# Four column groups for the router's product, and x's scale from sums on ScalarE

## The chip, the cores and the metric

The kernel runs on one core of one Trainium2 chip. The metric is device time in microseconds (us), the median of several executions. A core has TensorE (matmuls, written PE), VectorE (DVE), ScalarE (ACT), GpSimd (POOL) and SyncE (SP), which run their own instruction streams and meet at semaphores, and 16 DMA engines that they share.

## The reference

4096 tokens of 512 features pass through an adapted linear layer and then through a mixture-of-experts layer, with a residual:

```python
cond   = x @ W.T + ((x @ A[idx].T) @ Bm[idx].T) * scalings[idx]
shared = sum over 2 experts of gelu(cond @ Wsh_up[e]) @ Wsh_down[e]
probs  = softmax(cond @ W_router)                 # 512 x 16
gate   = the two largest of probs, zero elsewhere
routed = sum over 16 experts of gate[e] * gelu(cond @ Wrt_up[e]) @ Wrt_down[e]
out    = x + shared + routed
```

## The kernel before

The work has four stages: the linear layer with the router's logits, a shared-expert stage in which the tokens are also sorted by expert, the routed experts in 79 tiles of 128 tokens, and the rest of the shared experts with the sum of everything. The change lies in the first stage and its end.

The first stage goes over 16 chunks `c` of 256 tokens (`c = 2i + s`, where `s` picks one of two buffers), each of two tiles of 128 tokens. All matmuls but the router's, the adapters' second one and the transposes have two float16 parts for each float32 operand, `x` among them: `x` times a power of two is rounded to float16 (the high part, ScalarE, `high_x`), and what is left is the low part (VectorE, `x_low`); products run in three passes (high*high, high*low, low*high). The router's product is in float32, so that the choice of experts is right.

The first two chunks are an exception: their linear products are taken in float32, straight from the loaded weights.

TensorE's order is written out by hand. Step `c` (`cond_step`, L1301) is: `adapter_inputs(c)` (L1261), `cond_products(c, 0)` for the chunk's first tile (L1272), `cond_transposes(c-1)` (L1288), `cond_products(c, 1)`, `router_products(c-1)` (L1297), `adapter_products(c)` (L1280). The router's product takes 128 tokens of the transposed chunk `hid` as the stationary operand and 16 columns of the router's matrix `wr` as the moving one, four of them summed in PSUM for each tile. The routed weights, 16 experts, arrive by DMA in steps 0 to 6, and ScalarE and VectorE look for their scale in steps 0 to 7 (`lot_sums` with sums of absolute values at L643, `lot_maxima` at L881) and split them into parts in steps 8 to 15 (`high_routed` at L612, `low_routed` at L906, two experts in a step, each as an up and a down part).

The other engines' order in a step:

- ScalarE: `high_x(c+1)` (L654), `cond_T(c-1)` (L675, the transposes out of PSUM into `hid`), `lot_sums` or two `high_routed`, `cond_rows(c)` (L666, the linear layer's result out of PSUM into `rows`).
- VectorE: `mask_xa(c)` (L851), `row_max(c-1)` (L874), `x_low(c+1)` (L935), `x_largest` of chunk `c+2` (L918, then L920, which keeps the exponent), a weight piece, `x_scales(c+2)` (L925 to L929), a weight piece, `top(c-1)` (L859 to L869, the two best experts).
- GpSimd: one `partition_all_reduce` (L523) for chunk `c+2`, between `x_largest` and `x_scales`.
- SyncE: loads `x` of chunk `c+3`, up to two experts' weights, and stores `rows` and `hid`.

At the end of the stage SyncE reloads the first chunks of `hid` as `condT` for the shared experts (L394; chunk 1's load waits until all routed weights are split, since it lands behind them), ScalarE and VectorE split them (`high_condT` L633, `low_condT` L1002), and TensorE's order, after step 15, is: `shared_up` block 0 of chunk 0 (L1349), `cond_transposes(15)`, blocks 1 and 2, `router_products(15)`, block 3, block 0 of chunk 1, `prefix_products` (L1325), which needs the choice of experts of all tokens (VectorE's `top(15)` and one-hot matrices, L1050 to L1052).

## Time and profile before

| | us |
|---|---|
| median of 3 runs | 653.16 |
| lowest and highest | 651.33, 656.0 |
| the profiled execution | 656.53 |
| its span (first to last instruction) | 654.8 |
| mean granted clock of TensorE | 0.989 |

The profiled execution is one more run of the same program. Its span leaves out what lies before the first and after the last instruction, 1.73 us together. The rows of the trace come from it.

### The profile page before, as it was taken

The page shows a single profiled execution, that of the slowest core. Times are in us where ns is not written, and L with a number is a line of the kernel's source. Part 1 is how long each engine was busy: PE and PEld are TensorE (multiplying, and loading weights), DVE is VectorE, ACT ScalarE, POOL GpSimd, SP SyncE. Part 2 cuts the span into 40 slices and gives each one's busy share as a digit, 9 for nine tenths or more (in the row PEclk, how much of TensorE's full clock was granted, in tenths as well). Part 3 has the DMA queues.
Part 4 walks back from the last instruction along what each step waited for, and adds up shares of the span by engine and source line. Part 5 has one row for each costly group of instructions (what it writes and reads, how often), then busy time and mean ns, then how long its engine had stood idle before and what let it go on. Part 6 is the DMA issues. An engine that isn't in the chain of part 4 may idle for free.

```text
span 654.8 us, 13547 instructions
## 1 busy us (share of the span) xinstructions
PE 622.5 (95%) x4116; PEld 430.7 (66%) x4117; DVE 427.6 (65%) x820; ACT 323.4 (49%) x487; POOL 180.8 (28%) x270
## 2 busy tenths in 40 slices
PE   4999999999999999799999999999999998989794
PEld 2466666666676786477777777777777775756461
DVE  2768989999879963455555555555555534688774
ACT  0356567676766322255555555555555543333230
POOL 1000000000001002333333333333333227777770
PEclk8999999999999999999999999999999999999898
DMA  7699964444243423545555555555555459999976
GB/s 281 273 375 422 422 234 145 149 142 153 111 165 116 154 72 128 193 143 161 161 161 160 160 160 160 160 160 160 160 160 160 144 186 393 327 316 331 360 214 248
DMA packets 49477, 135.62 MB, mean 207 GB/s; under 512 B 6000, under 2 KB 6000, under 8 KB 47024
## 3 DMA queue, kind: packets, MB, share of 16 engines
q1 hardware_dynamic: 38016, 97.86, 39.9%
q0 software_dynamic: 11440, 37.50, 21.0%
q8 instruction: 11, 0.18, 0.1%
q14 instruction: 10, 0.08, 0.0%
HBM read 86.31 MB, written 49.02 MB: 207 GB/s over the span
## 4 chain that ended last, share of the span: by engine, by line
PE 71%; POOL 11%; DVE 6%; issue 6%; DMA 5%; ACT 1%; SPq 0%; POOLq 0%; DVEq 0%; ACTq 0%
PE bank L1440 16%; PE bank L1421 15%; PE bank L1272 12%; POOL rtw L579 10%; PE bank L1405 5%; PE bank L1280 4%; PE bank L1297 4%; PE bank L1261 3%; PE bank L1362 3%; PE bank L1430 3%; PE bank L1349 3%; PE bank L1288 2%; PE bank L1335 1%; DMA region<-w_r 1%; DMA rtw<-r_dram,row_idx 1%
## 5 line engine op out<-in xcount | busy, mean ns | idle before, releaser
L1149 DVE SCALAR_TENSOR_TENSOR region<-bank,scale,region 128x512 f16<-128x512 f32 x79 | 59.4, 751 | 114.1 <-ACT region L785 114.1
L1440 PE MATMUL bank<-rtw,tmp 128*128 x474 | 116.5, 382 | 3.0 <-DVE tmp L1157 3.0
L1421 PE MATMUL bank<-rtw,region 128*128 x948 | 116.6, 273 | 0.0
L1421 PEld LDWEIGHTS bank<-rtw,region 128*128 128x128 f16 x948 | 92.9, 98 | 10.2
L1362 PE MATMUL bank<-shw,hid 128*128 128x512 f16 x384 | 87.9, 384 | 8.5 <-DVE rtw L1216 7.8
L554 POOL DMA_INDIRECT region<-xc_dram,slot_idx x79 | 77.8, 985 | 61.3 <-POOL slot_idx L551 61.3
L1349 PE MATMUL bank<-act_in,shw 128*128 128x256 f16 x768 | 87.9, 273 | 1.7 <-issue 1.4
L1349 PEld LDWEIGHTS bank<-act_in,shw 128*128 128x128 f16 x768 | 74.8, 98 | 14.8 <-issue 2.2
L792 ACT ACTIVATE region<-bank,un_dn 128x512 f32<-128x512 f32 x79 | 54.3, 687 | 59.1 <-PE bank L1440 59.1
L579 POOL DMA_INDIRECT rtw<-r_dram,row_idx x64 | 71.5, 1117 | 27.8 <-issue 16.6
L1440 PEld LDWEIGHTS bank<-rtw,tmp 128*128 128x128 f16 x474 | 46.6, 98 | 42.1 <-issue 4.6
L1362 PEld LDWEIGHTS bank<-shw,hid 128*128 128x128 f16 x384 | 37.5, 99 | 52.5 <-DVE rtw L1216 6.9
L781 ACT ACTIVATE tmp<-bank,un_up 128x256 f32<-128x256 f32 x79 | 37.4, 474 | 64.3 <-PE bank L1421 64.3
L551 POOL COPY slot_idx<-tok 128x1 int32 (+1 forms) x79 | 15.3, 194 | 158.7 <-PE bank L1405 116.7
L785 ACT ACTIVATE region<-bank,scale 128x512 f16<-128x512 f32 x79 | 54.3, 687 | 6.0 <-PE bank L1405 6.0
L743 ACT ACTIVATE tmp<-bank,un_up 128x256 f32<-128x256 f32 x44 | 20.3, 471 | 72.0 <-PE bank L1349 52.9
L1191 DVE SCALAR_TENSOR_TENSOR rtw<-rtw,gate 128x512 f32 (+1 forms) x64 | 45.3, 749 | 14.8 <-DMA rtw<-r_dram,row_idx 10.2
L1405 PE MATMUL bank<-ident,region 128*128 128x128 f32 x316 | 47.5, 273 | 0.6 <-DMA region<-xc_dram,slot_idx 0.6
L906 DVE SCALAR_TENSOR_TENSOR rtw<-rtw,scale 128x1024 f16<-128x1024 f32 x32 | 39.7, 1280 | 6.5 <-ACT rtw L612 6.5
L1155 DVE TENSOR_SCALAR tmp<-bank,to_mid 128x256 f16<-128x256 f32 x79 | 38.2, 484 | 7.9 <-PE bank L1430 4.6
L523 POOL PARTITION_ALL_REDUCE x_max_all<-x_max x14 | 4.9, 352 | 128.2 <-DVE x_max L920 128.2
L1157 DVE SCALAR_TENSOR_TENSOR tmp<-bank,to_mid,tmp 128x256 f16<-128x256 f32 x79 | 38.2, 484 | 2.8
(156 smaller groups left out, 834.7 us busy)
## 6 DMA issues: line engine op xcount, KB each, us to landing
r_dram<-region SPq DMA_DIRECT2D x79, 256.0 KB
rtw<-rt_w SPq DMA_DIRECT2D x16, 1024.0 KB, 11.4
act_in<-xT SPq DMA_DIRECT2D x16, 512.0 KB, 4.1
xc_dram<-rows SPq DMA_DIRECT2D x16, 512.0 KB, 3.0
xcT_dram<-hid SPq DMA_DIRECT2D x16, 512.0 KB, 2.9
rtw<-x_rows SPq DMA_DIRECT2D x16, 512.0 KB, 4.5
rtw<-xcT_dram SPq DMA_DIRECT2D x13, 512.0 KB
out<-rtw SPq DMA_DIRECT2D x9, 512.0 KB
```

The lines of the kernel that those rows point to most:

```text
L554: nc.gpsimd.indirect_dma_start(out=xg[s], out_offset=None, in_=xc_dram, in_offset=bass.IndirectOffsetOnAxis(ap=slot_idx[s][:].bitcast(U32) ...
L579: nc.gpsimd.indirect_dma_start(out=routed_row(slot, r, t), out_offset=None, in_=r_dram, in_offset=bass.IndirectOffsetOnAxis(ap=row_idx[slo ...
L785: nc.scalar.activation(xgT[s][:, 0], R_XT[s][:].rearrange("p (k t) -> p k t", k=HK), ACT.Copy, scale=col(scale, C_ALL).bitcast(F32)).then_ ...
L792: nc.scalar.activation(rrow[s], R_DN[s][:], ACT.Copy, scale=col(un_dn, ROUTED)).then_inc(rrow_ready, 1)
L1149: nc.vector.scalar_tensor_tensor(xgT[s][:, 1], R_XT[s][:].rearrange("p (k t) -> p k t", k=HK), col(scale, C_ALL).bitcast(F32), xgT[s][:, 0 ...
L1191: last = nc.vector.scalar_tensor_tensor(y, routed_row(slot, r, t), gate[:, r, bass.ds(c * NT + t, 1)], y, ALU.mult, ALU.add)
L1272: last = mm(COND[NT * s + t][:], act_in[s][:, k, at] if whole else xp[s][:, ap, k, at], w_in[:, k, :] if whole else wt[:, bp, k, :], start ...
L1349: last = mm(UP[em % 2][:, 0:CHUNK], shw[:, e, w0:w0 + P], actT[s][:, xp, k, :], start=(k == 0 and n == 0), stop=(k == HK - 1 and n == 2))
L1362: last = mm(DOWN[t][:], hidT[s][:, xp, em, t * P:(t + 1) * P], shw[:, em // DM, w0:w0 + H], start=(em == 0 and n == 0), stop=(em == EM - 1 ...
L1405: last = nc.tensor.transpose(R_XT[s][:, k * P:(k + 1) * P], xg[s][:, k * P:(k + 1) * P], ident[:])
L1421: last = mm(R_UP[s][:, 0:D], xgT[s][:, xp, k, :], rtw[:, bass.ds(e, 1), w0:w0 + D].rearrange("p a d -> p (a d)"), start=(k == 0 and n == 0 ...
L1440: last = mm(R_DN[s][:], midT[s][:, xp, m, :], rtw[:, bass.ds(e, 1), w0:w0 + H].rearrange("p a h -> p (a h)"), start=(m == 0 and n == 0), s ...
```

## The change

The router's matrix becomes the stationary operand: each of its four pieces (128 features x 16 experts, padded with zeros to 32 columns) stands in column group `k` of the array, and the 256 tokens move. The four products are no longer summed in PSUM: product `k` writes PSUM partitions 32k to 32k+31 (`LOGIT_T`). ScalarE copies this to `lt` (`logit_T`), and a second product (`router_sums`, one for each tile of 128 tokens) with the constant matrix `fold` as moving operand sums the four groups and turns the result back to tokens x experts, for `top` as before. `router_sums(c-2)` stands behind `adapter_inputs(c)`, so `top(c-1)` of VectorE waits into TensorE's next step.

The scale of `x` no longer comes from the largest absolute value on VectorE but from the sum of absolute values of each partition on ScalarE (`x_sums`, in `cond_rows`), of which the largest over the partitions is taken as before; the exponent is now cut out behind GpSimd's reduction, by one more small operation in `x_scales`. `x_scales` and the weight pieces of VectorE change places. GpSimd pads `wr` with zeros, and the DMA that loads it now writes pieces of 64 bytes (16 columns of every 32) where it wrote 256 bytes for each partition. The parts of the diff that only size buffers and declare semaphores are left out (`GROUP` is 32, `fold` is 128 x 16, `lt` 128 x 256).

```diff
@@ -173,6 +175,8 @@
         ident = sb("ident", [P, P])
         lower = sb("lower", [P, P], BF16)
+        fold = sb("fold", [P, E_RT])
+        lt = sb("lt", [P, CHUNK])
         ones = sb("ones", [P, P], BF16)
         iota_p = xam[1][:].bitcast(F16).rearrange("p (l n) -> p l n", n=GRP // 2)
         iota_e = sb("iota_e", [P, E_RT])
...
@@ -243,6 +247,7 @@
         bank = [ctx.enter_context(nc.psum_tensor(f"bank{i}", [P, 512], F32)) for i in range(8)]
         XA, COND, XPOSE, LOGIT = bank[0], bank[1:3] + bank[6:8], bank[3:5], bank[5]
+        LOGIT_T, LOGIT = LOGIT[:, 0:CHUNK], LOGIT[:, CHUNK:CHUNK + NT * E_RT]
         PRE, TOT, INV, TILE_E = bank[6], bank[7], bank[0], bank[5]
         UP, DOWN = bank[1:3], bank[3:5]
         R_XT, R_UP, R_MT, R_DN = [bank[0], bank[5]], bank[6:8], bank[2:0:-1], bank[3:5]
...
@@ -339,7 +345,7 @@
             sp.dma_start(flat(act_in[0][:]), chunk_T(xT, 0)).then_inc(act_loaded[0], 16)
             sp.dma_start(sc_col[:], scal).then_inc(w_mask, 16)
             sp.dma_start(idx_b[:], idx.partition_broadcast(P)).then_inc(w_mask, 16)
-            for dst, src in ((w_in, WT), (bmt, BmT), (wr, w_r)):
+            for dst, src in ((w_in, WT), (bmt, BmT), (wr[:, :, 0:E_RT], w_r)):
                 sp.dma_start(dst, src).then_inc(w_cond, 16)
             sp.dma_start(flat(act_in[1][:]), chunk_T(xT, 1)).then_inc(act_loaded[1], 16)
             sp.dma_start(arrived(0), sh_up).then_inc(w_shared, 16)
@@ -502,6 +508,7 @@
                            allow_small_or_imprecise_dtypes=True).then_inc(iotas, 1)
             nc.gpsimd.iota(tok_no[:], [[P, TT]], base=-TOK // 2, channel_multiplier=1,
                            allow_small_or_imprecise_dtypes=True).then_inc(iotas, 1)
+            nc.gpsimd.memset(wr[:, :, E_RT:GROUP], 0.0).then_inc(wr_padded, 1)
             nc.gpsimd.memset(ident[:], 0.0).then_inc(masks, 1)
             nc.gpsimd.memset(ones[:], 1.0).then_inc(masks, 1)
             nc.gpsimd.memset(lower[:], 1.0).then_inc(masks, 1)
@@ -519,8 +526,8 @@
             def x_reduce(c, s):
-                pool.wait_ge(x_max_ready, c - 1)
-                nc.gpsimd.partition_all_reduce(x_max_all[s][:], x_max[s][:], P, RMAX).then_inc(x_reduced, 1)
+                pool.wait_ge(x_sum_ready, c - 1)
+                nc.gpsimd.partition_all_reduce(x_sum_all[s][:], x_sum[s][:], P, RMAX).then_inc(x_reduced, 1)
             reduce_max(1, LIN_W, SH_UP)
             reduce_max(2, SH_UP, RT_UP)
@@ -653,11 +660,19 @@
                 act.wait_ge(act_used, c - 1)
                 nc.scalar.activation(xp[s][:, 0], act_in[s][:], ACT.Copy, scale=x_scale[s][:].bitcast(F32)).then_inc(x_half, 1)
-            def cond_rows(i, s, first=False):
+            def x_sums(i, s):
+                act.wait_ge(act_loaded[s], 16 * (i + 2))
+                nc.scalar.activation(rows[s][:].rearrange("p t h -> p (t h)"), flat(act_in[s][:]), ACT.Abs,
+                                     accum_out=x_sum[s][:]).then_inc(x_sum_ready, 1)
+
+            def cond_rows(i, s, first=False, more=True):
                 c = 2 * i + s
                 if not first:
                     act.wait_ge(rows_stored[s], 16 * i)
                     act.wait_ge(c_chunk_ready, c - 1)
+                if more and not (first and s == 0):
+                    x_sums(i, s)
+                    act.wait_ge(x_sum_ready, c + 1)
                 for t in range(NT):
                     act.wait_ge(cond_ready, NT * c + t + 1)
                     if first:
@@ -675,25 +690,37 @@
                     nc.scalar.copy(hid[s][:, :, t * P:(t + 1) * P],
                                    XPOSE[t][:].rearrange("p (k t) -> p k t", k=HK)).then_inc(condT_ready, 1)
+            def logit_T(c, first=False):
+                act.wait_ge(lt_psum, c + 1)
+                if not first:
+                    act.wait_ge(logit_ready, c)
+                nc.scalar.copy(lt[:], LOGIT_T).then_inc(lt_ready, 1)
+
             def cond_step(i, s, first=False):
                 c = 2 * i + s
                 cond_T(c - 1, i - 1 + s, 1 - s, first)
+                logit_T(c - 1, first)
                 cond_rows(i, s, first and s)
             act.wait_ge(scale_ready, 1)
             high_linear(wt[:, 0], w_in, LIN_W)
             high_linear(at_[:, 0], at_in, LIN_A)
             cond_rows(0, 0, first=True)
+            act.wait_ge(act_loaded[0], 2 * 16)
+            nc.scalar.activation(hid[0][:].rearrange("p k t -> p (k t)"), flat(act_in[0][:]), ACT.Abs,
+                                 accum_out=x_sum[0][:]).then_inc(x_sum_ready, 1)
             high_x(2, 0)
             cond_step(0, 1, first=True)
             high_x(3, 1)
             cond_T(1, 0, 1, first=True)
+            logit_T(1)
             lot_sums(1)
             act.wait_ge(scale_ready, 2)
             high_shared(0)
             cond_rows(1, 0)
             high_x(4, 0)
             cond_T(2, 1, 0)
+            logit_T(2)
             lot_sums(3)
             high_shared(1)
             cond_rows(1, 1)
@@ -701,13 +728,14 @@
                 for s in range(2):
                     high_x(2 * i + s + 1, 1 - s)
                     cond_T(2 * i + s - 1, i - 1 + s, 1 - s)
+                    logit_T(2 * i + s - 1)
                     if i == 2:
                         lot_sums(5 + 2 * s)
                     else:
                         for e in (9 + 4 * s, 11 + 4 * s):
                             lot_sums(e)
                     cond_rows(i, s)
-            def routed_step(i, s, more=True):
+            def routed_step(i, s, more=True, more_x=True):
                 c = 2 * i + s
                 if more:
                     high_x(c + 1, 1 - s)
@@ -715,12 +743,14 @@
                     high_condT(0, 0, C_EARLY, early=True)
                     nc.scalar.activation(warm[:], sc_col[:], ACT.Gelu)
                 cond_T(c - 1, i - 1 + s, 1 - s)
-                for e in range(2):
-                    high_routed(2 * c - NC + e)
-                cond_rows(i, s)
+                high_routed(2 * c - NC)
+                logit_T(c - 1)
+                high_routed(2 * c - NC + 1)
+                cond_rows(i, s, more=more_x)
             high_x(NC // 2 + 1, 1)
             cond_T(NC // 2 - 1, A_HALF // 2 - 1, 1)
+            logit_T(NC // 2 - 1)
             act.wait_ge(scale_ready, 3)
             for e in range(2):
                 high_routed(e)
...
@@ -757,7 +787,9 @@
             gelus(0, 0, SH_FIRST, early=True, blocks=range(1))
             cond_T(NC - 1, A_HALF - 1, 1)
             high_condT(1, 1, C_EARLY, early=True)
-            gelus(0, 0, SH_FIRST, early=True, blocks=range(1, EM))
+            gelus(0, 0, SH_FIRST, early=True, blocks=range(1, 3))
+            logit_T(NC - 1)
+            gelus(0, 0, SH_FIRST, early=True, blocks=range(3, EM))
             high_hid(0, 0, SH_FIRST, early=True)
             gelus(1, 1, SH_FIRST, early=True, blocks=range(1))
             high_condT(2, 0, C_EARLY, early=True)
...
@@ -913,16 +945,12 @@
                 low(part(DN_LO), arrived(e + 1)[:, WU:], RT_DN, part(DN_HI), 2 * e + 4)
-            def x_largest(i, s):
-                dve.wait_ge(act_loaded[s], 16 * (i + 1))
-                nc.vector.tensor_reduce(x_max[s][:], flat(act_in[s][:]), AX_X, ALU.max, apply_absolute_value=True).then_inc(x_max_found, 1)
-                dve.wait_ge(x_max_found, 2 * i + s - 1)
-                nc.vector.tensor_scalar(x_max[s][:].bitcast(I32), x_max[s][:].bitcast(I32), 255 * EXP_ONE, None,
-                                        ALU.bitwise_and).then_inc(x_max_ready, 1)
-
             def x_scales(c, s):
                 dve.wait_ge(x_reduced, c - 1)
-                nc.vector.tensor_scalar(x_expo[s][:], x_max_all[s][:].bitcast(I32), float(30 * EXP_ONE), None,
+                nc.vector.tensor_scalar(x_expo[s][:], x_sum_all[s][:].bitcast(I32), 255 * EXP_ONE, None,
+                                        ALU.bitwise_and).then_inc(x_expo_found, 1)
+                dve.wait_ge(x_expo_found, c - 1)
+                nc.vector.tensor_scalar(x_expo[s][:], x_expo[s][:], float(30 * EXP_ONE), None,
                                         ALU.max).then_inc(x_expo_ready, 1)
                 dve.wait_ge(x_expo_ready, c - 1)
                 nc.vector.tensor_scalar(x_unscale[s][:], x_expo[s][:], float(-TOP * EXP_ONE), None, ALU.add)
@@ -947,20 +975,17 @@
                     mask_xa(c, s)
                 row_max(c - 1, 1 - s)
                 x_low(c + 1, 1 - s)
-                if masked:
-                    lot_maxima(lots[0])
-                x_largest(i + 1, s)
-                for at in lots[1:2] if masked else lots[0:1]:
+                for at in lots:
                     lot_maxima(at)
                 x_scales(c + 2, s)
-                for at in lots[2:] if masked else lots[1:]:
-                    lot_maxima(at)
                 top(c - 1, 1 - s)
             def low_linear(dst, src, n, hi, half):
                 dve.wait_ge(lin_half, half)
                 nc.vector.scalar_tensor_tensor(dst, src, col(scale, n).bitcast(F32), hi, ALU.mult, ALU.subtract).then_inc(lin_split, 1)
+            dve.wait_ge(consts, 1)
+            nc.vector.tensor_reduce(fold[:], ident[:].rearrange("p (k e) -> p e k", k=HK)[:, 0:E_RT, :], AX_X, ALU.add).then_inc(fold_ready, 1)
             mask_xa(0, 0)
             dve.wait_ge(w_cond, 3 * 16)
             dve.wait_ge(w_adapters, 16)
...
@@ -1025,14 +1049,12 @@
                 row_max(c - 1, 1 - s)
                 if c + 1 < NC:
                     x_low(c + 1, 1 - s)
-                if more:
-                    x_largest(i + 1, s)
                 if c + 1 == NC:
                     low_early(0)
                 low_routed(2 * c - NC)
+                low_routed(2 * c - NC + 1)
                 if more:
                     x_scales(c + 2, s)
-                low_routed(2 * c - NC + 1)
                 top(c - 1, 1 - s)
             for i in range(A_HALF // 2, A_HALF):
@@ -1292,14 +1314,20 @@
                 pe.wait_ge(condT_ready, NT * c + NT)
                 if not first:
                     pe.wait_ge(logit_copied, c)
+                for k in range(HK):
+                    last = mm(LOGIT_T[k * GROUP:(k + 1) * GROUP, :], wr[:, k, :], hid[s][:, k, :], start=True, stop=True)
+                last.then_inc(lt_psum, 1)
+
+            def router_sums(c):
+                pe.wait_ge(lt_ready, c + 1)
                 for t in range(NT):
-                    for k in range(HK):
-                        last = mm(LOGIT[:, t * E_RT:(t + 1) * E_RT], hid[s][:, k, t * P:(t + 1) * P], wr[:, k, :],
-                                  start=(k == 0), stop=(k == HK - 1))
+                    last = mm(LOGIT[:, t * E_RT:(t + 1) * E_RT], lt[:, t * P:(t + 1) * P], fold[:], start=True, stop=True)
                 last.then_inc(logit_ready, 1)
-            def cond_step(c, i, s, first=False):
+            def cond_step(c, i, s, first=False, sums=True):
                 adapter_inputs(c, i, s, whole=first)
+                if sums:
+                    router_sums(c - 2)
                 cond_products(c, s, 0, whole=first)
                 cond_transposes(c - 1, 1 - s, first)
                 cond_products(c, s, 1, whole=first)
@@ -1313,9 +1341,19 @@
             for t in range(NT):
                 cond_products(0, 0, t, whole=True)
             adapter_products(0, 0)
-            cond_step(1, 0, 1, first=True)
+            pe.wait_ge(wr_padded, 1)
+            pe.wait_ge(fold_ready, 1)
+            cond_step(1, 0, 1, first=True, sums=False)
             pe.wait_ge(lin_split, 2)
-            with pe.Fori(1, A_HALF) as i:
+            adapter_inputs(2, 1, 0)
+            router_sums(0)
+            cond_products(2, 0, 0)
+            cond_transposes(1, 1)
+            cond_products(2, 0, 1)
+            router_products(1, 1)
+            adapter_products(2, 0)
+            cond_step(3, 1, 1)
+            with pe.Fori(2, A_HALF) as i:
                 cond_step(2 * i, i, 0)
                 cond_step(2 * i + 1, i, 1)
@@ -1366,10 +1404,12 @@
             pe.wait_ge(w_split, 2)
             pe.wait_ge(rows_ready, TT - NT)
             shared_up(0, 0, first=True, blocks=range(1))
+            router_sums(NC - 2)
             cond_transposes(NC - 1, 1)
             shared_up(0, 0, first=True, blocks=range(1, 3))
             router_products(NC - 1, 1)
             shared_up(0, 0, first=True, blocks=range(3, EM))
+            router_sums(NC - 1)
             shared_up(0, 1, blocks=range(1))
             prefix_products()
             shared_up(0, 1, blocks=range(1, 3))
```

## Rows read from the trace of the kernel before

**Rows 1.** The profile page: busy time of each engine, and the DMA line of the 40 slices

```profile
PE 622.5 (95%) x4116; PEld 430.7 (66%) x4117; DVE 427.6 (65%) x820; ACT 323.4 (49%) x487; POOL 180.8 (28%) x270
...
DMA  7699964444243423545555555555555459999976
```

**Rows 2.** One step: length, PE, PEld, DVE, ACT, POOL busy us; clock, DMA share, GB/s

```profile
109.32:120.18 10.86, 10.86 (x67) 6.97 (x66) 10.21 (x24) 7.74 (x10) 0.35 (x1) 1.00 0.40 145
```

**Rows 3.** Chain that ended last, one step of the stage: start us, us, engine

```profile
109.32 1.69 PE bank L1297 x16
111.01 1.81 PE bank L1280 x4
112.82 1.31 PE bank L1261 x12
114.13 2.59 PE bank L1272 x12
116.72 0.87 PE bank L1288 x8
```

**Rows 4.** The same chain, the first steps

```profile
3.61 8.85 DMA region<-w_r
...
22.90 1.74 PE bank L1261 x8
...
31.97 0.97 ACT hid L675 x2
32.98 1.96 PE bank L1297 x16
```

**Rows 5.** TensorE in order of time (start us, us): the product with one stationary column

```profile
219.89 0.30 PE L1330 MATMUL bank<-ident,tile_col 128*1 128x82 f32 x2
220.13 2.79 PE L1349 MATMUL bank<-act_in,shw 128*128 128x256 f16 x24
```

**Rows 6.** Groups by line and shape, 0 to 260 us: busy us, mean ns, idle before

```profile
L918 DVE TENSOR_REDUCE x_max<-act_in 128x1 f32<-128x1024 f32 x14 | 17.0, 1214 | 7.1 <-DMA act_in<-xT 7.0
...
L743 ACT ACTIVATE tmp<-bank,un_up 128x256 f32<-128x256 f32 x24 | 10.9, 470 | 36.7 <-PE bank L1349 30.3 <-DVE hid L1010 6.4
L643 ACT ACTIVATE rtw<-rtw 128x1024 f16<-128x1024 f32 x10 | 10.5, 1057 | 0.2
```

**Rows 7.** ScalarE in order of time, one step

```profile
122.97 1.44 ACT L666 ACTIVATE rows<-bank,un_cond 128x512 f32<-128x512 f32 x2
124.31 1.14 ACT L654 ACTIVATE arena<-act_in,x_scale 128x1024 f16<-128x1024 f32 x1
128.06 1.07 ACT L675 COPY hid<-bank 128x512 f32<-128x512 f32 x2 [2.61 <-PE bank L1288]
```

**Rows 8.** TensorE in order of time, end of the stage

```profile
185.22 1.85 PE L1297 MATMUL bank<-region,hid 128*128 128x16 f32 x16
...
199.15 0.39 PE L1325 MATMUL bank<-arena,lower 128*128 128x512 bf16 x1 [1.13 <-DVE arena L1052]
```

**Rows 9.** ScalarE in order of time, end of the stage

```profile
185.92 2.35 ACT L612 ACTIVATE rtw<-rtw,scale 128x1024 f16<-128x1024 f32 x2 [0.32 <-DVE rtw L906]
...
194.59 0.82 ACT L743 ACTIVATE tmp<-bank,un_up 128x256 f32<-128x256 f32 x2
```

**Rows 10.** VectorE in order of time, end of the stage

```profile
184.60 4.98 DVE L906 SCALAR_TENSOR_TENSOR rtw<-rtw,scale 128x1024 f16<-128x1024 f32 x4 [2.07 <-ACT rtw L612]
...
195.92 0.18 DVE L859 COPY lg_c<-bank 128x32 f32<-128x32 f32 x1
...
197.21 1.42 DVE L1050 TENSOR_TENSOR arena<-iota_e,chosen 128x512 bf16<-128x512 f32 x2
```

**Rows 11.** SyncE's queue in order of time, end of the stage

```profile
189.61 0.35 SPq L394 DMA_DIRECT2D rtw<-xcT_dram  x1
```

**Rows 12.** VectorE in order of time, third step

```profile
47.67 1.22 DVE L918 TENSOR_REDUCE x_max<-act_in 128x1 f32<-128x1024 f32 x1 [5.03 <-DMA act_in<-xT]
```

**Rows 13.** ScalarE in order of time, third step

```profile
46.88 1.46 ACT L666 ACTIVATE rows<-bank,un_cond 128x512 f32<-128x512 f32 x2 [0.71 <-PE bank L1280]
```

More of the change, by code:

```diff
@@ L25 @@
 AR = N_AD * RANK
+GROUP = 32
+assert HK * GROUP == P and E_RT <= GROUP
 assert AR == P
@@ L124, in adaln_moe_kernel @@
         midT = [tmp[:, (2 + s) * D:(3 + s) * D].bitcast(F16).rearrange("p (a m t) -> p a m t", a=2, m=DM) for s in range(2)]
-        region = sb("region", [P, HK * H + HK * AR + H + HK * E_RT])
+        region = sb("region", [P, HK * H + HK * AR + H + HK * GROUP])
         def carve(sizes):
@@ L144, in carve @@
                 views.append(v)
-            assert at <= HK * H + HK * AR + H + HK * E_RT
+            assert at <= HK * H + HK * AR + H + HK * GROUP
             return views
-        wt, at_, bmt, wr = carve([((2, HK, H), F16), ((2, HK, AR), F16), ((H,), F32), ((HK, E_RT), F32)])
+        wt, at_, bmt, wr = carve([((2, HK, H), F16), ((2, HK, AR), F16), ((H,), F32), ((HK, GROUP), F32)])
         acc0, acc1, pref = carve([((TT, E_RT), F32)] * 3)
@@ L227, in adaln_moe_kernel @@
         un_up, to_mid, un_dn = sb("un_up", [P, 3]), sb("to_mid", [P, 3]), sb("un_dn", [P, 3])
-        x_max = [sb(f"x_max{s}", [P, 1]) for s in range(2)]
-        x_max_all = [sb(f"x_max_all{s}", [P, 1]) for s in range(2)]
+        x_sum = [sb(f"x_sum{s}", [P, 1]) for s in range(2)]
+        x_sum_all = [sb(f"x_sum_all{s}", [P, 1]) for s in range(2)]
         x_expo = [sb(f"x_expo{s}", [P, 1], I32) for s in range(2)]
@@ L261, in adaln_moe_kernel @@
         lin_half, lin_split = sem("lin_half"), sem("lin_split")
-        x_max_found, x_max_ready, x_reduced = sem("x_max_found"), sem("x_max_ready"), sem("x_reduced")
+        x_sum_ready, x_reduced, x_expo_found = sem("x_sum_ready"), sem("x_reduced"), sem("x_expo_found")
         x_expo_ready, x_scale_ready = sem("x_expo_ready"), sem("x_scale_ready")
@@ L270, in adaln_moe_kernel @@
         logit_ready, logit_copied, best_ready = sem("logit_ready"), sem("logit_copied"), sem("best_ready")
+        wr_padded, fold_ready, lt_psum, lt_ready = sem("wr_padded"), sem("fold_ready"), sem("lt_psum"), sem("lt_ready")
         place_found, top_ready = sem("place_found"), sem("top_ready")
@@ L732, in _ @@
             for s in range(2):
-                routed_step(A_HALF - 1, s, more=s == 0)
+                routed_step(A_HALF - 1, s, more=s == 0, more_x=False)
             def gelus(c, s, n=SH_REST, early=False, blocks=range(EM)):
@@ L858, in top @@
                 dve.wait_ge(logit_ready, c + 1)
-                nc.vector.tensor_copy(lg_c[s][:], LOGIT[:, 0:NT * E_RT].rearrange("p (t e) -> p t e", t=NT)).then_inc(logit_copied, 1)
+                nc.vector.tensor_copy(lg_c[s][:], LOGIT.rearrange("p (t e) -> p t e", t=NT)).then_inc(logit_copied, 1)
                 dve.wait_ge(logit_copied, c + 1)
@@ L981, in _ @@
             link(nc.vector.tensor_scalar(mask[:], mask[:], w_to_a[:], None, ALU.mult))
-            x_largest(1, 0)
             x_scales(2, 0)
```

## The prediction

> **What bounds the kernel now.** I read the page first: TensorE is busy 95% of the span and no other engine passes 66% [rows 1]. Since that is an average over four stages, I then took busy time by stretch for one step of the stage that changes. A step lasts 10.87 us; TensorE is busy for all of it, VectorE for 10.2 us and ScalarE for 7.7 us [rows 2]. So TensorE sets the pace and VectorE stands 0.65 us behind it: a saving on TensorE alone would soon stop at VectorE. The chain of waits says the same: it runs through TensorE's five pieces of a step without a gap, 1.69 (router) + 1.81 (adapters) + 1.31 + 2.59 twice + 0.87 (transposes) = 10.86 us [rows 3]. Two places are not TensorE's: in steps 0 to 5 the DMA engines are nearly full as well (nines in the slices from 33 to 82 us [rows 1]), and at the end of the stage the chain goes through ScalarE, VectorE and a DMA before it comes back to TensorE [rows 8 to 11].
>
> **TensorE, the first router product.** Removed: 16 records in 1.69 us, one per 106 ns [rows 3]: each of 8 float32 products is two records, and each streams only 16 columns, so the stationary loads set the time. Added: 4 products with 256 moving columns, 8 records. The trace has this very shape with the full array, the adapters' float32 product of chunk 1: 8 records of 256 columns in 1.74 us, 0.218 us a record [rows 4]. That is the upper bound, if the groups don't overlap: the streamed columns cost more than the loads that were saved. The lower bound is two records, 0.44 us, if all four groups run together. No row of the trace shows two matmuls at once. I take 5 records, 1.09 us, by this mechanism: the two records of a product use the same columns of the array and can't overlap; if records start in the order of the program, group 1's first starts beside group 0's second, and so on, so each further product adds one record: 2+1+1+1. It lies between the ends, and I choose it since the records of this trace on TensorE always start in program order.
>
> The page "TensorE: Matmul & The Clock Gate" of the Trainium skill, Part 3, says that matmuls on different column groups run concurrently with starts about 4 ns apart, and that matmuls nevertheless start and end in strict order. No run here shows either yet; the first half of the rule alone would make the product about one product long, the lower bound, and the second half is what speaks for 5 records.
>
> **TensorE, the second product and the switches.** `router_sums` is 2 float32 products, 4 records with 128 stationary columns, 16 moving: at 106 ns each [rows 3] 0.42 us. Going into the grouped form and out of it may cost time too. The nearest row is the product with one stationary column: two records of 82 columns, which at 256 columns in 0.218 us need 0.14 us, but the next line starts 0.24 us after them [rows 5]. I take these 0.10 us for each switch, 0.20 us a step, with 0 and 0.3 us a step as bounds.
>
> The page "TensorEngine Tiling (Array Packing)" of the Trainium skill, under Key Properties, says that changing the tiling mode drains TensorE. It gives no time; the 0.10 us of that row agree with its direction, and the sum doesn't need the rule.
>
> Step: -1.69 + 1.09 + 0.42 + 0.20 = +0.02 us. Up to the transposes of chunk 14, where the end of the stage takes over, there are 14 of them: +0.3 us.
>
> **VectorE and ScalarE in the steps.** VectorE loses the largest value, 1.21 us [rows 6], and its mask goes to x_scales: some 9.0 us are left of 10.87. ScalarE gains x_sums: 1.06 us [rows 6] and some 0.2 us to read the accumulator; and logit_T, 128x256 out of PSUM, 0.47 us like the GELU of that shape [rows 6]: 7.7 + 1.7 = 9.4 us. Both fit. What matters is the new wait on ScalarE: logit_T stands between the two high_routed and waits for the router's product, and x_sums stands ahead of cond_rows. From the product's end E: 0.1 + 0.42 (copy) + 2.3 (second high_routed) + 1.25 (x_sums) + 0.1 + 1.34 (rows [rows 7]) puts `rows` at E+5.5. The transposes that need them start after the switch, 1.81 + 1.31 + 0.42 + 2.59 us [rows 3], at E+6.2: 0.7 us of slack, where before the idle of 2.6 us ahead of the copies [rows 7] and more was there. Then high_x takes it to E+6.6, before the next transposes are out. VectorE: x_scales wait for the sums (E+4.5), top(c-1) for router_sums; x_low follows high_x (E+6.6) and row_max and is out at some E+9.0, while adapter_inputs need it at E+12.7. Cost nothing, as long as the 0.7 us hold.
>
> GpSimd's reduction is as long as before and still has no one but x_scales behind it. SyncE's queue is unchanged in order; its stores follow `rows` and `hid`, up to 2 us later in a step, hidden, since the same buffer is written again two steps (21.7 us) on.
>
> **The first steps.** The load of w_r ends the wait for the first products (8.85 us [rows 4]); it now writes 512 pieces where there were 128, 24 more for each DMA engine: some 0.3 us, 0 to 0.5. On the other side, router(0) waited until 32.98 for the copies that stood behind x's scale on VectorE [rows 4]; ScalarE can sum chunk 2 while VectorE still splits weights: -0.6 us. Chunk 4's x lands at 47.67, behind the routed weights [rows 12]; rows(2) were copied at 46.88 [rows 13] and now stand behind the sum of chunk 4: 47.7 + 1.25 + 0.1 + 1.34 = 50.3. The transposes of chunk 2 came at 51.36 and come at some 50.7 now: no wait. With 0.65 us less a step they would come at 49 and lose about 1 us.
>
> **The end of the stage.** The chain there: the last low_routed (184.60, four, to 189.5 [rows 10]), the DMA of chunk 1 (189.61 [rows 11]), its high part, the GELU of block 1 (to 195.0 [rows 9]), block 3. The second pair of high_routed started at 185.92 [rows 9]. Now it waits for logit_T(14): the product starts at 185.22 [rows 8], + 0.1 + 1.09 + 0.1 + 0.42 = 186.95, so the last low_routed, the DMA and the GELU are 0.9 us later: 195.9. Then block 3, 1.31; router_sums(15) with a switch, 0.52; top(15), which had started at 195.92 [rows 10], now only here: 1.3; the one-hot matrices, 1.9 [rows 10]: 201.0. prefix_products started at 199.15 with 1.13 us of waiting [rows 8]. +1.8 us. The 0.6 + 0.6 us that the two last router products may save here are swallowed by that wait. Everything behind it hangs on TensorE and moves along.
>
> **Sum:** 0.3 + 0.3 - 0.6 + 1.8 = +1.8 us, on the profiled execution 656.5 to 658.3. That execution lies 3.4 us over the median of 653.16; on the median: 655.0. Its own range, from no switches and no cost of the load (-2.8 - 0.3) to 0.3 us of switches and 2 us more at the end: 651 to 659.
>
> **Rivals.** (1) The four groups overlap wholly: 0.44 us in place of 1.09, 0.65 us less a step, 14 steps: -9.1, and the end 0.6 us less late, against 1 us lost at the transposes of chunk 2: 646.3, without switches 643.5. For it: the groups share neither columns nor PSUM partitions. Against it: two records for each product, in order. It is only to be had since VectorE, at 9.0 us, now fits under a step of 10.2. (2) Slower: the groups don't overlap at all, so that the change doesn't do what it says. 8 records, 1.74 us: +0.65 us a step, +9.1, and 0.6 us more at the end: 664.7, without switches 662. It decides from the point where the records of the product take over 1.3 us. For it: every matmul of this trace has the array alone. (3) ScalarE becomes the bound: if its waits add more than 0.7 us between E and rows, TensorE waits for `rows` ahead of each transposes. Price for 0.5 us over it, in the 6 steps with both high_routed and x_sums: +3 us, 658; it can come on top of each case.
>
> **Chances.** The forecast 0.38, whole overlap 0.32, none 0.25, ScalarE's bound 0.05. A run of this kernel tells about 1% (6.5 us) from no change. Faster by over 1% (under 646.6): a bit over half of the first rival, 0.2. Slower by over 1% (over 659.7): the second and the edge of the third, 0.28. Within 1%: 0.52. The range goes from 644 to 665, since the bounds of the unknown overlap lie that far apart and neither rival can be left out.
>
> **What would show it.** The distance from the start of the grouped products to adapter_products: 0.5, 1.1 to 1.2 or 1.8 us. A step of 10.2, 10.9 or 11.6 us. ScalarE's copy of `lt` about 0.1 us behind the product's end; no idle of TensorE ahead of the transposes but for chunk 2; prefix_products' wait grown from 1.1 to over 2 us. The forecast is wrong first of all if the records of one product overlap each other or if those of different groups don't, next if a switch costs several tenths.

## The result, and the profile after

The changed kernel takes 652.51 us (median of 12 runs, 648.17 to 655.01). The kernel before, run 12 times beside it, takes 654.11 us (650.85 to 657.67). The ratio is 0.9958, with an interval of 0.9939 to 0.9977: some 2.7 us faster (the medians lie 1.6 us apart). The forecast was 655.0, a slight loss; the time lies inside its range, and on the other side of no change. The profiled execution has a span of 651.2 us.

The page after, busy time by engine:

```profile
PE 615.5 (95%) x4052; PEld 410.8 (63%) x4053; DVE 412.5 (63%) x807; ACT 341.9 (53%) x531; POOL 181.5 (28%) x271
```

TensorE has lost 7.0 us of busy time and VectorE 15.1, ScalarE has gained 18.5 [rows 1]; the share of TensorE is still 95%. The chain of waits, one step, as in [rows 3] (start us, us, engine; the first row is the high part of the step before):

```profile
126.76 2.59 PE bank L1294 x12
129.35 0.57 PE bank L1318 x8
129.92 1.91 PE bank L1302 x4
131.83 1.31 PE bank L1283 x12
133.14 0.35 PE bank L1324 x4
133.50 2.60 PE bank L1294 x12
136.10 0.87 PE bank L1310 x8
```

The chain still runs through TensorE alone. The router's 1.69 us [rows 3] have become 0.57 (grouped products) and 0.35 (router_sums), and adapter_products read 1.91 for 1.81. The chain counts from end to end; by starts adapter_products are as long as before (1.82 and 1.80 us), and the 0.09 us stand ahead of the product. The step is 10.21 us, 0.66 less. Busy time by stretch of that step, columns as in [rows 2]:

```profile
129.92:140.13 10.21, 10.21 (x62) 5.64 (x61) 9.55 (x24) 9.12 (x12) 0.50 (x1) 1.00 0.44 155
```

TensorE is full; VectorE's busy time fell from 10.21 us [rows 2] to 9.55 (9.2 to 9.6 in the steps after it), and it still fits, 0.66 us under the step.

Fourteen steps of 0.66 and 0.7 us at router(0) would be some 10 us. To see where they went I follow the starts of the transposes. TensorE in order of time, before: transposes of chunk 0 and of chunk 14, first matmul of the routed stage:

```profile
27.90 1.04 PE L1288 MATMUL bank<-ident,rows 128*128 128x128 f32 x8
...
181.76 1.04 PE L1288 MATMUL bank<-ident,rows 128*128 128x128 f32 x8
...
275.11 2.74 PE L1440 MATMUL bank<-rtw,tmp 128*128 x6 [3.03 <-DVE tmp L1157]
```

And after, with the three that wait longest between them (in brackets the idle time ahead and what ended it):

```profile
29.34 1.04 PE L1310 MATMUL bank<-ident,rows 128*128 128x128 f32 x8
...
92.96 1.16 PE L1310 MATMUL bank<-ident,rows 128*128 128x128 f32 x8 [0.54 <-ACT rows L681]
...
104.00 1.16 PE L1310 MATMUL bank<-ident,rows 128*128 128x128 f32 x8 [0.54 <-ACT rows L681]
...
115.39 1.16 PE L1310 MATMUL bank<-ident,rows 128*128 128x128 f32 x8 [0.90 <-ACT rows L681]
...
176.77 1.04 PE L1310 MATMUL bank<-ident,rows 128*128 128x128 f32 x8
...
272.90 1.77 PE L1480 MATMUL bank<-rtw,tmp 128*128 x6 [3.02 <-DVE tmp L1179]
```

The stretch from chunk 0 to chunk 14 fell from 153.86 to 147.43 us, 6.4 and not 10: in the steps 2 to 8 TensorE waits for ScalarE's `rows`. From chunk 14 to the routed stage it grew from 93.35 to 96.13 us, 2.8 us given back. The rest is not the change's: the routed stage itself lasts as long (256.2 us in both up to the start of the last stage), and the last stage, which no edit touches, lasted 120.4 to 125.3 us in the profiles of this study (130.0 in e1, whose choice of experts is another).

ScalarE in the step of the first of these waits:

```profile
86.32 0.37 ACT L697 COPY lt<-bank 128x256 f32<-128x256 f32 x1 [2.49 <-PE bank L1318]
86.59 1.06 ACT L650 ACTIVATE rtw<-rtw 128x1024 f16<-128x1024 f32 x1
...
90.98 1.04 ACT L665 ACTIVATE rows<-act_in 128x1024 f32<-128x1024 f32 x1
...
92.15 1.27 ACT L681 ACTIVATE rows<-bank,un_cond 128x512 f32<-128x512 f32 x2
```

`logit_T` stands first in this step, so ScalarE idles 2.49 us for the product and only then takes four weight pieces (lot_sums) and x_sums; `rows` come 5.83 us behind the start of the copy. In a step from chunk 9 on, where a high_routed stands ahead of `logit_T` and only one behind it, they come after 4.01 us:

```profile
129.99 0.37 ACT L697 COPY lt<-bank 128x256 f32<-128x256 f32 x1 [0.45 <-PE bank L1318]
130.60 2.24 ACT L619 ACTIVATE rtw<-rtw,scale  x2 [0.24 <-DVE rtw L938]
132.75 1.04 ACT L665 ACTIVATE rows<-act_in 128x1024 f32<-128x1024 f32 x1
...
134.00 1.27 ACT L681 ACTIVATE rows<-bank,un_cond 128x512 f32<-128x512 f32 x2
```

The end of the stage, TensorE in order of time:

```profile
188.01 0.64 PE L1318 MATMUL bank<-hid,region 128*32 128x256 f32 x8
191.51 2.28 PE L1387 MATMUL bank<-act_in,shw 128*128 128x256 f16 x12 [2.85 <-ACT tmp L773]
193.58 0.87 PE L1324 MATMUL bank<-fold,lt 128*128 128x16 f32 x4
...
197.72 0.39 PE L1363 MATMUL bank<-arena,lower 128*128 128x512 bf16 x1 [1.43 <-DVE arena L1074]
```

Then the DMA that reloads chunk 1, in the chain of waits, first as it was before, then after:

```profile
189.61 3.90 DMA rtw<-xcT_dram
184.99 4.83 DMA rtw<-xcT_dram
```

Last, two windows of that stretch, with the granted clock in the third column from the end:

```profile
189.00:192.00 3.00, 0.49 (x5) 0.48 (x6) 0.97 (x1) 2.14 (x4) 0.00 (x0) 1.00 0.95 338
192.00:195.00 3.00, 3.00 (x17) 2.37 (x16) 0.80 (x5) 1.02 (x2) 0.00 (x0) 0.50 0.36 146
```

prefix_products start 20.95 us behind the transposes of chunk 14; before it was 17.39 (199.15 [rows 8] less 181.76). Three things stand in these rows: a wait of 2.85 us for the GELU; behind it a granted clock of 0.50, the 1.2 GHz level, after 3 us in which TensorE was busy for 0.49; and, by that clock, 2.28 us for a block that takes 1.47 and 0.87 for sums that take 0.52. Ahead of the wait stands the DMA of 4.83 us, 0.93 longer than before.

### The profile page after: what moved, and what is told of

Read it like the earlier page. It is cut to its first block, busy times and chain, and to the rows that moved or that the text cites. A ratio compares the mean times of both kernels' runs of the same rounds, so it can differ in the third digit from the quotient of the medians.

```text
span 651.2 us, 13468 instructions
## 1 busy us (share of the span) xinstructions
PE 615.5 (95%) x4052; PEld 410.8 (63%) x4053; DVE 412.5 (63%) x807; ACT 341.9 (53%) x531; POOL 181.5 (28%) x271
## 4 chain that ended last, share of the span: by engine, by line
PE 70%; POOL 11%; issue 6%; DMA 5%; ACT 4%; DVE 3%; SPq 0%; POOLq 0%; DVEq 0%; ACTq 0%
PE bank L1480 16%; PE bank L1461 16%; PE bank L1294 11%; POOL rtw L586 10%; PE bank L1445 5%; PE bank L1387 4%; PE bank L1400 4%; PE bank L1302 3%; PE bank L1470 3%; PE bank L1283 2%; PE bank L1310 2%; PE bank L1373 1%; DMA rtw<-r_dram,row_idx 1%; DMA region<-w_r 1%; PE bank L1318 1%
## 5 line engine op out<-in xcount | busy, mean ns | idle before, releaser
L530 POOL PARTITION_ALL_REDUCE x_sum_all<-x_sum x14 | 7.1, 508 | 131.0 <-ACT rows L665 127.9
```

## The experiments

Each is set against the changed kernel unless it says otherwise; ratios are against the kernel before, run beside it (0.9958 for the changed kernel).

**Do the groups overlap, and by which rule? (e1, e2, e9)** The three kernels of this part also copy to `lt` only the partitions that are written, and set the rest of it to zero once. They leave out part of the features, so the choice of experts is another, and their whole times are not comparable; their steps are. All four products into one column group:

```
-    mm(LOGIT_T[k * GROUP:(k + 1) * GROUP, :], wr[:, k, :]
+    mm(LOGIT_T[0:GROUP, :], wr[:, k, :]
```

> The four grouped products all go to column group 0 (each overwrites the one before, so only the last quarter of the features reaches the logits; the rest of lt is zero). Theory (products overlap only across different groups): 8 records one after the other at 0.22 us, 1.75 us from the first to adapter_products in place of 0.57, and TensorE's step rises from 10.2 to 11.4 us. Rival (a narrow product of 32 columns is quick by itself, whatever the group): the 0.57 us and the 10.2 us stay.

Two groups, in the order 0, 1, 0, 1 (`k % 2` in place of `k`):

> The products go to groups 0, 1, 0, 1 (half of the features reach the logits). Theory (each group has its own line of work, records of different groups run side by side): 4 records deep, 0.87 to 1.0 us to adapter_products. Rival (only records next to each other in the program can overlap, the order of starts is kept): 5 to 6 records deep, 1.1 to 1.3 us.

Two groups, in the order 0, 0, 1, 1 (`k // 2` in place of `k`):

> As with two groups, but in the order 0, 0, 1, 1 (half of the features reach the logits). Theory (every column group has its own line of work, and a record waits for its own group alone): again 4 records deep, 0.99 us from the first grouped product to adapter_products, as in the order 0, 1, 0, 1. Rival (a record can't start before those ahead of it in the program): group 1's first record starts beside group 0's fourth, 7 records deep, 1.5 to 1.65 us.

TensorE in order of time, one step of each; first e1:

```profile
140.38 1.91 PE L1321 MATMUL bank<-hid,region 128*32 128x256 f32 x8
142.23 1.98 PE L1305 MATMUL bank<-region,xam 128*128 128x512 f32 x4
```

then e2:

```profile
132.87 1.06 PE L1321 MATMUL bank<-hid,region 128*32 128x256 f32 x8
133.86 1.98 PE L1305 MATMUL bank<-region,xam 128*128 128x512 f32 x4
```

then e9:

```profile
132.51 1.06 PE L1321 MATMUL bank<-hid,region 128*32 128x256 f32 x8
133.50 1.98 PE L1305 MATMUL bank<-region,xam 128*128 128x512 f32 x4
```

From product to adapter_products: 1.85, 0.99 and 0.99 us, where the changed kernel has 0.57; steps of 11.49, 10.63, 10.63 and 10.21. At 0.218 us a record [rows 4] these are 8, 4, 4 and 2 records, and 0.11 to 0.13 us more. So the gain needs different groups (e1 undoes it and the step is 0.6 us longer than before the change), and the time is that of the fullest group. e9 settles the rule: if records had to start in the order of the program, 0, 0, 1, 1 would have been 7 deep; it is 4. A record waits for its own group alone. The starts of single records say the same. The trace doesn't name a record's group, but in e1, with one group, records start 0.22 to 0.24 us apart, so two that start together are in different groups. The rows of the first 0.1 us of e9's product and of the changed kernel's (the last number is the records started so far):

```profile
132.51 0.42 PE L1321 MATMUL bank<-hid,region 128*32 128x256 f32 x2
129.28 0.42 PE L1318 MATMUL bank<-hid,region 128*32 128x256 f32 x4
```

In e9 two records start 0.014 us apart, then two more 0.24 us later: the third product, of group 1, starts ahead of the second, of group 0. In the changed kernel four start within 0.02 us, and the other four 0.24 us behind them. The one run of e1 took 678.04 us, that of e2 660.33, of e9 657.96.

**The groups without x's sums (e3), and the sums without the groups (e4).** e3 leaves VectorE's largest value and takes x_sums off ScalarE; e4 leaves the router as it was before.

```
 e3:  -   cond_rows(i, s, more=more_x)      ScalarE: no x_sums ahead of rows
      +   cond_rows(i, s)                   VectorE: tensor_reduce(x_max, ..., abs max) as before
 e4:      only x_sums on ScalarE, its accumulator read by x_scales; router_products as before
```

> The router's part of the change alone; x's largest value stays on VectorE. Theory: VectorE's 10.2 to 10.4 us of work in a step of 10.2 us becomes the bound in steps 8 to 13, at 10.5 to 10.9 us a step (2 to 4 us in all), while ScalarE's stalls ahead of the transposes of chunks 2, 3, 6 and 7 (2.2 us) vanish: 0 to 2 us slower than the whole change, ratio to before 0.996 to 0.999. Rival: VectorE was never near the bound, and without ScalarE's stalls it is faster than the whole change, ratio under 0.994.

> x's scale from sums on ScalarE alone; the router as before. Theory: TensorE's step of 10.87 us holds, ScalarE has over 0.7 us to spare since it doesn't wait for lt; only the first router product comes 0.6 us earlier: ratio 0.998 to 1.000. Rival: x_sums ahead of cond_rows stall the transposes here too (chunks 2, 6 and 7, 1 us or more): ratio over 1.001.

e3: 653.82, ratio 0.9959 (0.9931 to 0.9988), the same as the whole change. Chunk 0 to chunk 14 takes 145.38 us, 8.5 less than before: the steps are 10.21 us up to chunk 9, with no wait for `rows`, and 10.32 to 10.55 after that. Windows of such a step of e3, columns as in [rows 2]:

```profile
133.06:143.61 10.55, 10.49 (x62) 5.54 (x61) 10.16 (x24) 7.69 (x12) 1.31 (x1) 1.00 0.40 150
```

VectorE is busy for 10.16 of 10.55 us, and the chain of waits of such steps runs through VectorE and at most one high_routed of ScalarE: VectorE is the bound there, as the idle time of 0.65 us before the change [rows 2] said it would be. At router(0), TensorE waits for ScalarE's copies to `hid`, which stand behind high_x and so behind VectorE's scale of x:

```profile
34.02 0.64 PE L1319 MATMUL bank<-hid,region 128*32 128x256 f32 x8 [0.62 <-ACT hid L682]
```

e4: 655.75, ratio 0.9986 (0.9963 to 1.0009). Steps stay at 10.87, and the first one is 0.88 us shorter. By themselves the sums bring nothing that the times tell from no change, and no transposes wait for `rows` in e4. In the change they buy what e3 lacks at router(0) and in the late steps, and pay for it with `rows` being late in steps 2 to 8: it takes both, `logit_T` ahead of the weight pieces and x_sums behind them.

**The waits for `rows` (e6).** One call of lot_sums, two weight pieces, now goes ahead of `logit_T` in steps 2 to 7 (in short):

```
-                    logit_T(2 * i + s - 1)
-                    ... lot_sums of this step
+                    lot_sums(5 + 2 * s if i == 2 else 9 + 4 * s)
+                    logit_T(2 * i + s - 1)
+                    if i > 2:
+                        lot_sums(11 + 4 * s)
```

(likewise in steps 2 and 3, and in step 8 one high_routed of the two)

> The changed kernel with logit_T behind the first of ScalarE's weight pieces in steps 2 to 8, as it stands already in steps 9 to 15. Theory (ScalarE idles some 2.5 us a step in front of lt and then is late with rows): the waits ahead of the transposes of chunks 3, 6, 7 and 8 vanish but for the one that x's arrival sets (chunk 2), 2.5 to 3 us earlier at the transposes of chunk 14, ratio to before 0.991 to 0.993. Rival (those waits come from VectorE or from the DMA load of x): they stay, ratio 0.995.

647.84, ratio 0.9922 (0.9891 to 0.9953). TensorE, chunks 0, 8 and 14, then the end of the stage:

```profile
28.80 1.04 PE L1308 MATMUL bank<-ident,rows 128*128 128x128 f32 x8
...
111.32 1.04 PE L1308 MATMUL bank<-ident,rows 128*128 128x128 f32 x8
...
172.58 1.04 PE L1308 MATMUL bank<-ident,rows 128*128 128x128 f32 x8
...
186.06 1.47 PE L1385 MATMUL bank<-act_in,shw 128*128 128x256 f16 x12 [1.61 <-ACT tmp L771]
...
191.16 0.39 PE L1361 MATMUL bank<-arena,lower 128*128 128x512 bf16 x1 [1.95 <-DVE arena L1072]
```

143.78 us from chunk 0 to chunk 14: 10.08 less than before, 3.65 less than in the changed kernel. The waits are gone, that of chunk 2 too, which had been put down to x's arrival. The time alone doesn't part e6 from the changed kernel (the intervals touch), but e11 and e5 below, which differ by this edit alone, stand apart. prefix_products follow 18.58 us behind the transposes of chunk 14, with no halved clock in between, though this kernel's end is written as in the changed one.

**The end of the stage (e5).**

```
-            high_condT(1, 1, C_EARLY, early=True)
-            gelus(0, 0, SH_FIRST, early=True, blocks=range(1, 3))
             logit_T(NC - 1)
+            high_condT(1, 1, C_EARLY, early=True)
 TensorE: router_sums(15) ahead of block 3; VectorE: top(15) ahead of low_early(1)
```

> The changed kernel with the end of the stage put in another order: logit_T(15) ahead of high_condT(1) on ScalarE, router_sums(15) ahead of shared_up's block 3 on TensorE, top(15) ahead of low_early(1) on VectorE. Theory (the 3.6 us lost at the end come from top(15) standing behind the reload of chunk 1, block 3 and the sums): prefix_products start 3 to 3.5 us earlier, at some 17.5 us behind the transposes of chunk 14 in place of 20.95, ratio to before 0.990 to 0.992. Rival (the end is bound by the reload of chunk 1 and the shared products behind it, whatever the choice of experts does): TensorE waits elsewhere, under 1 us gained, ratio 0.995.

650.04, ratio 0.9943 (0.9923 to 0.9963), not told apart from the changed kernel. TensorE of e5:

```profile
188.91 0.62 PE L1323 MATMUL bank<-fold,lt 128*128 128x16 f32 x4 [0.49 <-ACT lt L697]
190.96 4.45 PE L1386 MATMUL bank<-act_in,shw 128*128 128x256 f16 x24 [1.42 <-ACT tmp L773]
195.24 0.38 PE L1362 MATMUL bank<-arena,lower 128*128 128x512 bf16 x1
```

prefix_products start 18.70 us behind the transposes of chunk 14, 2.2 earlier than in the changed kernel but no earlier than in e6. The clock was halved here too (24 matmuls in 4.45 us, where it takes 2.78). So e5 doesn't bear out that the order costs the 3.6 us: two thirds of that are the slow DMA and the halved clock of one execution; e6 and e7, with the changed kernel's order, have 18.58 and 18.33 (e9, e3 and e2, with that order as well and other steps, some 18.8, 19.3 and 19.6).

**The load of the router's matrix (e7).** w_r is padded to 32 columns in DRAM, so that a partition is one contiguous piece and GpSimd's memset goes.

> The changed kernel with the router's matrix padded to 32 columns in DRAM, so that its load writes 512 bytes for each partition in one piece. Theory (the 64-byte pieces cost the 0.6 us by which the first products started later): w_r lands 0.6 us earlier, 8.8 us from its issue, ratio 0.995 to 0.996, hardly told apart from the whole change. Rival (the 0.6 us vary from run to run with the load of the weights ahead of it): 9.5 us stay.

651.89, ratio 0.9969 (0.9948 to 0.9990), not told apart from the changed kernel. The products whose wait the load ends start at 12.45 us; with pieces of 64 bytes they started at 12.19 to 13.92 in nine profiles (13.13 in that of the changed kernel, most of them near 12.85), with contiguous ones at 12.38, 12.45, 12.50 and 12.91. Some 0.3 us may be there, under the scatter. What this run showed besides is the clock again, here behind prefix_products (194.68, after a wait of 1.96 us). Windows of e7, the clock in the third column from the end:

```profile
192.00:195.00 3.00, 1.04 (x9) 0.60 (x7) 2.83 (x11) 0.86 (x1) 0.00 (x0) 1.00 0.25 53
195.00:198.00 3.00, 3.00 (x17) 2.01 (x15) 2.92 (x6) 1.53 (x3) 1.91 (x2) 0.54 0.82 326
```

A halved stretch costs 1.7 us in TensorE's own rows: 24 matmuls take 4.45 us in place of 2.78 here, in e3 and in e5, and two blocks and the sums of the changed kernel add up to the same, 0.5 us of it hidden by the wait behind them. How much of that reaches the routed stage is not shown: from prefix_products to there e7 and e3 take 77.1 and 77.4 us, e5, e6, e8 and the changed kernel 75.2 to 75.4, but e10, with no halved clock, 77.1 too. Such a stretch stands at the end of the stage in four profiles (changed kernel, e3, e5, e7) of the eight with a step of 10.2 us, and in none of the five others (before, e1, e2, e4, e9).

**Combinations (e8, e10, e11).** e8 is e5, e6 and e7 together; e11 is e5 and e6; e10 is e3 with the end of e5, to see what x's sums bring once the rest is mended.

> The three edits together. Theory: they lie one after the other on TensorE's path and add up, 6 to 7 us under the whole change, ratio to before 0.985 to 0.987. Rival: an earlier stage end is given back at the sort or at the start of the routed tiles (the gathers wait for xc and the sort): ratio over 0.990.

> The router's part alone, x's largest value on VectorE, with the new order at the end of the stage (chunk 15's sums and choice of experts first). Theory: against the three edits together it loses 0.7 us at the first router product and 0.9 us in steps 9 to 14, where VectorE sets the pace, and so is 1.6 us slower: ratio to before 0.990 to 0.992. Rival (moving x's scale to ScalarE is worth nothing once ScalarE's order is right): ratio 0.988 to 0.989.

> The edits of ScalarE's order and of the end of the stage, with the router's load as in the change (64-byte pieces). Theory: the load costs about 0.3 us, so the ratio to before is that of the three edits together within 0.001: 0.988 to 0.990. Rival (the padding gave a microsecond or more): ratio 0.991 or more.

| | time | ratio | interval | chunk 0 to 14 |
|---|---|---|---|---|
| e8 | 645.74 | 0.9884 | 0.9857 to 0.9910 | 143.77 |
| e11 | 645.99 | 0.9871 | 0.9837 to 0.9905 | 143.78 |
| e10 | 648.83 | 0.9900 | 0.9866 to 0.9933 | 145.39 |

TensorE of e8 at the end of the stage:

```profile
185.48 0.62 PE L1320 MATMUL bank<-fold,lt 128*128 128x16 f32 x4 [0.49 <-ACT lt L696]
186.98 1.47 PE L1382 MATMUL bank<-act_in,shw 128*128 128x256 f16 x12 [0.89 <-ACT tmp L770]
...
190.43 0.39 PE L1358 MATMUL bank<-arena,lower 128*128 128x512 bf16 x1 [0.30 <-DVE arena L1070]
```

With no halved clock, prefix_products follow 17.33 us behind chunk 14's transposes (190.43 less 173.10): 1.25 less than in e6, which is what the order is worth there. e11 has 17.33 as well, with a DMA of 4.47 us for chunk 1 where e6 has 3.59, so with the new order a slow DMA of that size doesn't reach prefix_products. e8 missed what was expected, 6 to 7 us under the changed kernel: by the ratios it is 4.8 us, and the rows give 3.65 and 1.25. Both versions with e5 and e6 beat the two kernels of this case; the padding adds nothing that can be measured. In the trace x's sums are worth 1.6 us (143.8 against 145.4), 0.7 of it at router(0) and 0.9 in the late steps, while the intervals of e10 and the other two overlap.

## Why the prediction was wrong

**The grouped products: the step that failed.** The sum went by 5 records, 1.09 us. Measured: 0.57 us from the first record to adapter_products, two records (0.44) and 0.13 for the switch. The reason given, that records start in program order and so each further product adds one, is refuted by e9. The two rows that it rested on showed matmuls that all use the full array; they could not speak of matmuls in different groups. This term alone is 0.65 us a step, 9.1 us: it is rival 1's mechanism (0.63 us a step less than before by its sum, 0.66 measured).

The Trainium skill, "TensorE: Matmul & The Clock Gate", Part 3, says that matmuls on different tiles of the array run concurrently; the 0.57 us and the four starts within 0.02 us agree with it. The same section says that matmuls start and end strictly in program order. e2 and e9 differ only in that order and take the same 0.99 us, so for the length of the product the measurement decides against that half, which I had let weigh.

**The terms beside it** held. router_sums: 0.35 to 0.37 us where 0.42 was said. Switches: 0.13 us out of the form and some 0.09 at the entry (2.68 us from the start of the high part to the product, where the part takes 2.59), 0.22 to 0.23 a step against 0.20. router(0): 0.88 us came from the sums alone (e4), 0.6 was said.

**ScalarE's wait: the second step that failed.** It was put at nothing, and weighed for the steps with both high_routed only. There it held: `rows` end at 135.27, 5.4 us behind the product's end at 129.85, where 5.5 was worked out, and the transposes start at 135.93, 6.1 behind it (those of the first tile need only the first of the two copies, so the slack is larger than the 0.7 us). Left out were the steps 2 to 8, where `logit_T` stands ahead of all weight pieces. Rival 3 named the mechanism (one more wait of ScalarE makes `rows` late) and gave 0.05 to the wrong steps; there it cost 3.65 us, shown by e6. The whole overlap didn't bring this wait on: both `rows` and the transposes are counted from the product's end, so the length of the step cancels. e1, with 8 records and steps of 11.48 us, has the same waits in the same steps, 3.4 us in all, the longest here:

```profile
125.22 1.16 PE L1313 MATMUL bank<-ident,rows 128*128 128x128 f32 x8 [0.86 <-ACT rows L682]
```

So the forecast with 5 records would have had to carry them too. Chunk 2's wait, put at 1 us for a step of 10.2 and at x's arrival, was 0.2, and none in e6.

**VectorE** was said to be the limit of a saving on TensorE alone; e3 shows it, but at a price of 0.9 us and not more, since only the late steps grew, by 0.11 to 0.34 us each. With the sums on ScalarE its busy time in a step is 9.2 to 9.6 us, not 9.0.

**The end of the stage** was put at +1.8 us, or +1.2 with whole overlap. In e6 and e7, which have the same end and no halved clock ahead of prefix_products, it is +1.2 and +0.9. In the profile of the changed kernel it is +3.6, and the difference is the DMA of 4.83 us and the clock behind the wait. The clock was in no term of the sum: after waits of 1.4 to 2.9 us at this place TensorE's granted clock was sometimes 0.50 for some 3 us. Of the four kernels with the new order one profile (e5) shows it, of the other four three do: too few to say that the order prevents it.

**The load of w_r**, +0.3, is neither shown nor excluded.

**From the terms to the time.** With whole overlap, 0.65 us × 14, the sum of the prediction gave 646.3. Measured is 652.5. Of the 6 us between them, 3.65 are the waits for `rows`, against which 1 had been set down. Another 0.95 is the starting point: twelve runs put the kernel before at 654.11, and the sum started from three at 653.16. The halved clock, 1.7 us in half of the profiles, would be some 0.9 on average, an estimate. The rest, some 1.7 us, isn't settled. That 655.0 lies only 2.5 us off is luck: the product's gain of 9.1 us was missing from the sum, and so were these losses. Every version's time fell by less than its steps did: e6 saves 10.1 us up to chunk 14 and gives back 1.2, and its ratio makes 5.1 us (3.1 to 7.1); e11 saves 10.1 and makes 8.4 (6.2 to 10.7). A profile is one execution: before's first products (L1272) took 8.68 us, where the other profiles have 8.8 to 9.9, e4 with the same router and load among them at 9.7; and the routed stage took 254.7 (e8) to 257.6 us (e3), though no edit touches it.

## What to carry to other kernels

Small float32 products whose stationary side is 32 columns or less are worth putting in different column groups: they cost as many records as the fullest group has, whatever the order, and 0.22 us for going in and out. What the form brings is what is left after the second product: here 1.69 us became 0.57, 0.09 and 0.35. A copy that waits for TensorE belongs, on the engine that copies, behind some work that is ready and not ahead of all of it: ScalarE's 2.5 us of idle time ahead of `lt` cost 3.65 us in all, though ScalarE was busy for half of the span. When a step gets shorter, work out for every kind of step which producer has the least slack, not for the kind that was looked at first: a wait that is counted from the start of the same product doesn't depend on how long the step is.

## What the runs showed of the hardware

A record in one column group doesn't wait for an earlier record in another: 0, 0, 1, 1 and 0, 1, 0, 1 both take 0.99 us, and in 0, 0, 1, 1 the first records of both groups start 0.014 us apart. The two records of a float32 product do follow each other inside their group: four groups take two records' time, not one. TensorE's granted clock stood at 0.50 for some 3 us after TensorE had waited 2.85 us, and likewise in e7 after waits of 1.35 and 1.96 that ended 5.1 us apart; it stayed at 1.00 in e6 after 1.61 and 1.95, 5.1 us apart too, so nearly the same waits don't always cost it. A load in 512 pieces of 64 bytes shows no cost over the scatter, which is 0.5 us for the load in whole rows.
